# First self-attention: side jobs split over tiles, fewer and larger gathers; cross-attention value and mask jobs at other key tiles

## The reference

```python
x = x + _L0_attn_ref(_layernorm(x), ...)       # 16 heads of 16, ALiBi-like bias
x = x + _L0_xattn_ref(_layernorm(x), ctx_768, mask, ...)   # 8 heads of 64, 1601 keys, masked
x = x + _L0_ffn_ref(_layernorm(x), ...)
x = x + _L1_attn_ref(_layernorm(x), ...)
x = x + _L1_xattn_ref(_layernorm(x), ctx_768, ...)         # 16 heads of 64, 1601 keys
x = x + _L1_ffn_ref(_layernorm(x), ...)

def _L0_attn_ref(x, in_proj_weight, in_proj_bias, out_proj_weight, out_proj_bias):
    qkv = x @ in_proj_weight.T + in_proj_bias
    q, k, v = ...                                # 4 x 16 x 512 x 16 each
    bias = jnp.minimum(rel[None, :, :] * slopes[:, None, None], MAX_BIAS)
    scores = jnp.einsum('bhqd,bhkd->bhqk', q, k) * D ** (-0.5) + bias[None]
    probs = jax.nn.softmax(scores, axis=-1)
    out = jnp.einsum('bhqk,bhkd->bhqd', probs, v)
    return out.transpose(0, 2, 1, 3).reshape(B, S, C) @ out_proj_weight.T + out_proj_bias
```

## Time and profile before

| what | us |
|---|---|
| median of 3 runs (lowest, highest) | 3209.64 (3207.70, 3210.42) |
| the profiled execution | 3209.26 |
| its span, first to last instruction | 3207.5 |
| TensorE busy in the span | 2823.4 (88%) |
| VectorE, ScalarE, GpSimd busy | 1851.7, 1302.5, 1648.4 |
| mean granted TensorE clock | 0.947 |

### The profile page before, as it was taken

How to read it: one execution, slowest core, us unless ns; L and a number is a source line. 1 busy time by engine, 2 the same in 40 slices (tenths; PEclk the granted TensorE clock), 3 DMA queues, 4 the chain that set the end, 5 groups by cost and what they waited for, 6 DMA issues and landing times. The chain is left out here.

```text
span 3207.5 us, 38273 instructions
## 1 busy us (share of the span) xinstructions
PE 2823.4 (88%) x12634; PEld 1744.4 (54%) x12634; DVE 1851.7 (58%) x3753; ACT 1302.5 (41%) x2326; POOL 1648.4 (51%) x1404
## 2 busy tenths in 40 slices
PE   6578786899999999688899999999999999999979
PEld 5333344556565565354655655565556556566457
DVE  2356675566666666536555655555565565565556
ACT  1134554444444454311444444444444444444410
POOL 0344402566566666610466665666666666666710
PEclk8778998999999999898899999999999999999979
DMA  8666513232232322100332232232322233222110
GB/s 266 157 167 151 142 15 90 54 99 67 63 89 64 90 58 56 35 0 22 102 73 49 64 101 49 68 73 58 90 66 67 55 99 75 49 67 63 31 53 27
DMA packets 113532, 245.81 MB, mean 77 GB/s; under 512 B 15366, under 2 KB 61703, under 8 KB 112184
## 3 DMA queue, kind: packets, MB, share of 16 engines
q1 hardware_dynamic: 107128, 219.82, 27.6%
q0 software_dynamic: 5696, 23.42, 2.7%
q10 hardware_dynamic: 512, 0.13, 0.0%
HBM read 107.31 MB, written 31.76 MB: 43 GB/s over the span
## 5 line engine op out<-in xcount | busy, mean ns | idle before, releaser
L1009 POOL TENSOR_TENSOR ACC<-ACC,PR 128x512 f32<-128x512 f32 (+1 forms) x1056 | 1331.1, 1283 | 486.2 <-ACT PR L1234 476.8
L1234 ACT ACTIVATE PR<-banks 128x512 f32<-128x512 f32 (+1 forms) x832 | 469.1, 597 | 682.6 <-PE banks L1123 681.2
L1295 DVE TENSOR_REDUCE mx<-banks 128x2 f32<-128x800 f32 (+1 forms) x512 | 504.2, 986 | 406.8 <-PE banks L1075 405.6
L1139 PE MATMUL banks<-PR,V 128*64 128x512 f32 (+1 forms) x2496 | 602.5, 607 | 0.0
L1122 PE MATMUL banks<-QA,KA 128*128 128x512 f32 (+1 forms) x1248 | 535.4, 429 | 9.7 <-DMA QB<-ROW 8.7
L1075 PE MATMUL banks<-KH,QZ 128*128 128x400 f32 (+1 forms) x1536 | 482.7, 372 | 58.2 <-DVE mx L1295 37.9
L1123 PE MATMUL banks<-QB,KB 65*128 65x512 f32 (+1 forms) x1248 | 495.0, 397 | 0.0
L1075 PEld LDWEIGHTS banks<-KH,QZ 128*128 128x128 f32 x1536 | 268.3, 189 | 246.5 <-issue 113.6
L1234 ACT ACTIVATE PR<-banks,small 128x512 f32<-128x512 f32 (+1 forms) x416 | 269.3, 687 | 306.5 <-PE banks L1123 298.8
L1292 DVE CUSTOM_DVE_ANT_0 banks<-banks,maskadd 128x400 f32<-128x400 f32 (+1 forms) x512 | 289.9, 588 | 158.5 <-PE banks L1075 153.0
L1263 DVE TENSOR_TENSOR KB<-banks,KH 64x400 fp32r<-64x400 f32 (+1 forms) x384 | 219.4, 571 | 261.4 <-ACT KH L1167 255.9
(11 more groups left out here) (240 smaller groups left out, 3047.0 us busy)
## 6 DMA issues: line engine op xcount, KB each, us to landing
KA<-KH SPq DMA_DIRECT2D x192, 400.5 KB, 6.7
CX<-ctx_split SPq DMA_DIRECT2D x8, 2403.0 KB, 10.7
WK<-wk_split SPq DMA_DIRECT2D x48, 256.0 KB, 5.7
WV<-wv_split SPq DMA_DIRECT2D x24, 512.0 KB, 3.6
QA<-QZ SPq DMA_DIRECT2D x96, 128.0 KB, 2.3
QB<-QZ SPq DMA_DIRECT2D x96, 128.0 KB, 2.4
first<-in_w_in SPq DMA_DIRECT2D x8, 1024.0 KB, 6.0
second<-in_w_out1T SPq DMA_DIRECT2D x8, 1024.0 KB, 8.7
```

Source lines behind the costliest of these rows:

```text
L1009: pool.tensor_tensor(acc, other, PR[0:r, n % RING, :], ALU.add).then_inc(summed, 1)
L1139: last = pe.matmul(OB[h * DH:(h + 1) * DH, :], V[0:r, g % 4, s, h * DH:(h + 1) * DH], PR[0:r, (n + h) % RING, :], start=(s == 0), stop=(s ...
L1234: act.activation(PR[0:r, n % RING, :], SB[n % 3][0:r, :], ACT.Exp, bias=keybias[0:r, g // pairs, t:t + 1] if masked else 0.0).then_inc(pro ...
L1295: dve.tensor_reduce(mx[:, :, t, c], couples[i % 2 if g == 0 else 0][:, :, 0:w], AX.X, ALU.max).then_inc(mx_done, 1)
```

## The change

It has six parts.

1. **Jobs split over tiles.** Of a job at tile n, TensorE's part stays at n; ScalarE's copy of the job bank comes one tile later, its rounding to HI two tiles later; VectorE's LO comes four tiles later and its part of v and o jobs two tiles later, and all of VectorE's job parts now stand after the tile's maximum. VectorE normalises at tile 9 of a group and not at 7.
2. **Jobs at other tiles:** p at 0, 4, 20, 29; v at 45, 48; a at 13, 16; o at 32, 36; turn at 7; row at 10. LEAD is 24. The first batch's v jobs stand before its third and fourth p job.
3. **Larger gathers.** The weights' columns are reordered on the host (`paired`), so that the four heads of a half lie side by side. `parts` now has a place for each of the three parts, HI is written twice, and each side of a half is gathered by two transfers of 48 rows, queries first.
4. TensorE's first jobs stand ahead of its wait for the row loads (`self_in`).
5. GpSimd starts to split only after the first group's row has arrived.
6. **Cross-attention:** four value jobs stand at t = 4, 5, 7, 9 and three at 5, 7, 9; the seven stay. The mask steps stand at t = 11 (first), 12 (second and third) and 13 (fourth).

```diff
-        self.parts = nc.dram_tensor("parts", (2, 2, 4, P, S), F32).ap()
+        self.parts = nc.dram_tensor("parts", (2, 4, 2, 3, DH, S), F32).ap()
...
-        HALF = 12 * 16
+        HALF = 4 * 16
...
-                jobs += {1: [("p", b + 1, 0)], 3: [("p", b + 1, 1)], 17: [("p", b + 1, 2)], 19: [("p", b + 1, 3)],
+                jobs += {0: [("p", b + 1, 0)], 4: [("p", b + 1, 1)], 20: [("p", b + 1, 2)], 29: [("p", b + 1, 3)],
...
-                            for side in range(2):
+                            for side, kinds in ((0, "hlh"), (1, "hhl")):
                                 i = 4 * b + 2 * half + side
-                                c = 2 * side + half
-                                sp.wait_ge(lo_ready, i + 1)
+                                to = self.parts[b % 2, 2 * side + half]
                                 if b >= 2:
                                     sp.wait_ge(stacked[half], HALF * (b - 1))
-                                sp.dma_start(self.parts[b % 2, 0, c], raw(HI[:, i % 2, :])).then_inc(hl_out[i % 2], 16)
-                                sp.dma_start(self.parts[b % 2, 1, c], raw(LO[:, i % 2, :])).then_inc(hl_out[i % 2], 16)
-                            for side in range(2):
-                                sp.wait_ge(hl_out[side], 32 * (2 * b + half + 1))
+                                sp.wait_ge(hi_ready, i + 1)
+                                for blk in range(3):
+                                    if kinds[blk] == "h":
+                                        sp.dma_start(to[:, blk], raw(HI[:, i % 2, :])).then_inc(hl_out[i % 2], 16)
+                                sp.wait_ge(lo_ready, i + 1)
+                                sp.dma_start(to[:, kinds.index("l")], raw(LO[:, i % 2, :])).then_inc(hl_out[i % 2], 16)
                             if b >= 2:
                                 sp.wait_ge(sc_ready, PB * (b - 1))
-                            for side, to, parts in ((1, KS, (0, 0, 1)), (0, QS, (0, 1, 0))):
-                                for blk, part in enumerate(parts):
-                                    src = self.parts[b % 2, part, 2 * side + half].rearrange("(i two d) n -> two d i n", two=2, d=D)
-                                    for par in range(2):
-                                        o = DH * par + D * blk
-                                        sp.dma_start(raw(to[o:o + D, b % 2, 4 * half:4 * half + 4, :]), src[par]).then_inc(stacked[half], 16)
+                            for side, to in ((0, QS), (1, KS)):
+                                sp.wait_ge(hl_out[side], 48 * (2 * b + half + 1))
+                                for par in range(2):
+                                    src = self.parts[b % 2, 2 * side + half, par].rearrange("k (d i) n -> (k d) i n", d=D)
+                                    sp.dma_start(raw(to[DH * par:DH * par + 48, b % 2, 4 * half:4 * half + 4, :]), src).then_inc(stacked[half], 16)
...
                     pieces = self.split_pieces()
+                    pool.wait_ge(row_in, 32)
...
+                    for x in before():
+                        job(x)
                     pe.wait_ge(self.self_in, 16 * 8)
                     pe.wait_ge(ones_made, 2)
-                    for x in before():
-                        job(x)
...
-                            act.wait_ge(job_done, i + 1)
-                            act.activation(HI[:, j % 2, :], FULL[:, j % 2, :], ACT.Copy).then_inc(hi_ready, 1)
...
+                    def rounded(x):
+                        j = 4 * x[1] + x[2]
+                        act.wait_ge(job_done, place[x] + 1)
+                        act.activation(HI[:, j % 2, :], FULL[:, j % 2, :], ACT.Copy).then_inc(hi_ready, 1)
...
-                        for x in at(n):
+                        for x in at(n - 2) if n >= 2 else []:
+                            if x[0] == "p":
+                                rounded(x)
+                        for x in at(n - 1) if n >= 1 else []:
                             job(x)
...
-                        for x in at(n):
-                            job(x)
                         if n + LEAD < N:
                             maxima(n + LEAD)
-                        if n % GN == 7 and g >= 1:
+                        for x in at(n - 4) if n >= 4 else []:
+                            if x[0] == "p":
+                                job(x)
+                        for x in at(n - 2) if n >= 2 else []:
+                            if x[0] in "vo":
+                                job(x)
+                        if n % GN == 9 and g >= 1:
...
-            if t >= 4:
-                jobs += values_at(g)[t - 4:t - 3]
+            todo = values_at(g)
+            for x, tile in zip(todo, {0: (), 3: (5, 7, 9), 4: (4, 5, 7, 9), 7: range(4, 11)}[len(todo)]):
+                if tile == t:
+                    jobs.append(x)
...
-                            if masked and g % pairs == 1 and g // pairs + 1 < B and t in (0, 11, 12, 13):
-                                mask_step(g // pairs + 1, (0, 11, 12, 13).index(t))
+                            if masked and g % pairs == 1 and g // pairs + 1 < B:
+                                for c in {11: (0,), 12: (1, 2), 13: (3,)}.get(t, ()):
+                                    mask_step(g // pairs + 1, c)
```

More of the change, by code:

```diff
@@ L403, in self_attention @@
         PB = H * NT
-        LEAD, RING = 22, 8
+        LEAD, RING = 24, 8
         ROWS = 63
         SB, MB, OB, JB = bank[0:3], bank[3:6], bank[6], bank[7]
-        HALF = 12 * 16
+        HALF = 4 * 16
         ident = self.ident
@@ L423, in before @@
         def before():
-            return [("p", 0, i) for i in range(4)] + [("v", 0, 0), ("v", 0, 1)]
+            return [("p", 0, 0), ("p", 0, 1), ("v", 0, 0), ("v", 0, 1), ("p", 0, 2), ("p", 0, 3)]
         def at(n):
@@ L430, in at @@
             if b + 1 < B:
-                jobs += {1: [("p", b + 1, 0)], 3: [("p", b + 1, 1)], 17: [("p", b + 1, 2)], 19: [("p", b + 1, 3)],
-                         34: [("v", b + 1, 0)], 37: [("v", b + 1, 1)]}.get(l, [])
+                jobs += {0: [("p", b + 1, 0)], 4: [("p", b + 1, 1)], 20: [("p", b + 1, 2)], 29: [("p", b + 1, 3)],
+                         45: [("v", b + 1, 0)], 48: [("v", b + 1, 1)]}.get(l, [])
             if b >= 1:
-                jobs += {13: [("a", b - 1, 0)], 15: [("a", b - 1, 1)], 25: [("o", b - 1, 0)], 29: [("o", b - 1, 1)]}.get(l, [])
-            if n % GN == 6 and n >= GN:
+                jobs += {13: [("a", b - 1, 0)], 16: [("a", b - 1, 1)], 32: [("o", b - 1, 0)], 36: [("o", b - 1, 1)]}.get(l, [])
+            if n % GN == 7 and n >= GN:
                 jobs.append(("turn", n // GN - 1, 0))
-            if n % GN == 11 and n // GN + 1 < NG:
+            if n % GN == 10 and n // GN + 1 < NG:
                 jobs.append(("row", n // GN + 1, 0))
@@ L693, in job @@
                             if j >= 2:
-                                dve.wait_ge(hl_out[j % 2], 32 * (j // 2))
+                                dve.wait_ge(hl_out[j % 2], 48 * (j // 2))
                             dve.tensor_tensor(LO[:, j % 2, :], FULL[:, j % 2, :], raw(HI[:, j % 2, :]), ALU.subtract).then_inc(lo_ready, 1)
@@ L1853, in flat, with paired @@
         return g[name].reshape(-1)
+    def paired(w):
+        w = w.copy()
+        w[..., 0:2 * C] = w[..., 0:2 * C].reshape(-1, 4, H // 4, 2, D).transpose(0, 1, 3, 4, 2).reshape(w[..., 0:2 * C].shape)
+        return w
     mask = g["mask_BxS2_bk0"]
@@ L1860, in layouts @@
         "mask": mask, "maskT": padded.reshape(B, KT, P).transpose(0, 2, 1),
-        "w0_in": g["L0_attn_in_proj_weight"].T, "b0_in": g["L0_attn_in_proj_bias"],
-        "b0_cols": g["L0_attn_in_proj_bias"][0:2 * C].reshape(4, P).T,
+        "w0_in": paired(g["L0_attn_in_proj_weight"].T), "b0_in": g["L0_attn_in_proj_bias"],
+        "b0_cols": paired(g["L0_attn_in_proj_bias"])[0:2 * C].reshape(4, P).T,
         "w0_out": g["L0_attn_out_proj_weight"].T, "b0_out": g["L0_attn_out_proj_bias"],
```

4 lines of the change are left out of this document (3 added, 1 removed).

## The result

The changed kernel takes 3235.8 us (median; the kernel before, on the same chip, 3207.9 us): a ratio of 1.0088, with a 95% interval from 1.0063 to 1.0112. It is slower by about 28 us. I had forecast 3227 us. One of its seven executions took 9202.7 us and is left out of the ratio.

The account below looks back on a forecast made before the run. The self-attention tile loop was taken as a chain through three score banks, the cross-attentions as nearly full on TensorE. 3209 us, +48 for self-attention (slow writes in place of a 48 us gain), -30 for cross-attention: 3227 us, 8-in-10 range 3150 to 3285.

Parts of the forecast that it names:

- Two engines: Self-attention's scratch writes of 2x64 rows would run on two DMA engines, 5.5 us a write where it is 0.7.
- The chain of writes sets the last batch's tile 8: Last half of the weights in place at 504 us, making the last batch's tile 8 in self-attention 51 us late.
- two engines, but hidden: Rival: self-attention's slow writes delay only the lead-in, as halves are needed late; 3157 us, chance 0.18.
- All else would be 48 us faster: Lead-in and self-attention loop gain 48 us together if each transfer were as quick as before.
- The lead-in's term: Before the first tile: earlier first projection, earlier gathers, two more maxima ahead; -10 us (-6 to -13).
- The loop's terms: Self-attention tile loop: projections, value and output jobs, turns and row waits, -38 us.
- Turns: Self-attention loop: TensorE no longer stands before a turn for ScalarE's raised outputs; 15 at 0.65 us, -10 us.
- Row waits: Self-attention loop: TensorE's waits for the row transfer beside a gather go; -10 us (-3 to -14).
- Projections: Self-attention loop: the 12 projections inside it delay the tiles less, over three batches; -13 us (-8 to -26).
- The last batch gains 3 us: Self-attention's last batch, from its late tile 8 to the stage's end at 522, gains 3 us.
- Cross-attention: Both cross-attentions: moved mask copy and value jobs give -30 us (-22 to -38).
- what was to show it: Signs: maxima start near 162 us, waits for parts' writes and gathers, last batch's tile 8 near 504, shorter cross-attention groups.

Follow-up runs that it names:

- quick writes: Changed kernel with each write to the scratch tensor cut into two of 64 rows: 3213.8 us, ratio 1.0025 to the kernel before.
- the old rows: Changed kernel with the scratch tensor, writes (128 rows) and gathers (16 rows) of the kernel before: 3203.4 us, ratio 0.9988.
- the early turn: Changed kernel with turn at tile 6, normalise at 7, output jobs at 31 and 34 (were 7, 9, 32, 36): 3217.4 us, ratio 1.0022.
- the kernel with two of its parts: The kernel before with the two cross-attention edits and the lead-in's new job order: 3164.2 us, ratio 0.9867.

## Why the prediction came out as it did

The time is right to 9 us, and so is the sign. But its two large terms are wrong by 74 and 88 us, in opposite directions.

1. *Two engines.* Right: 4 completion packets and 12.7% of 16 engines. The rule of the Trainium skill (DMA: Bandwidth & Descriptors, "Why a DMA increments its semaphore by 16 and not by 1") gives 2 for these writes, and the trace agrees.
2. *The chain of writes sets the last batch's tile 8, +51 us there.* This step failed, although its number looks right: the last half landed at 484.2 us (504 forecast), and the tile is at 497.4 (504 forecast). But with quick writes the loop up to that tile is no shorter, 301.3 us against 299.6. Landing 13 us ahead of its use, the chain ended no wait there. In the profile it shows in the loop as 4.2 us of TensorE's waits, at tile 8 of the first batch, and 4.8 us of ScalarE's, at three of its twelve copies, where I had expected three in each batch. Measured, the writes cost 22 us, all of it in the lead-in (and 42 us by the medians, 30 by the profiled spans, once the tiles are quicker). That is the rival *two engines, but hidden*, which I gave 0.18 and priced at 3157 us. The chain itself was priced fairly: 363 us from the first write to the last landing, where the sum had 380, and 46 us from one half's landing to the next, over the 44 us that I had named as the bound. But I compared it with tiles as quick as before: a batch took 95 to 103 us and not 79, in which two halves of 46 us have room.
3. *All else would be 48 us faster.* Wrong, the larger error: with quick writes I had put 3131 us, and the kernel with writes of 64 rows takes 3213.8. The lead-in's term holds: 164.7 for 173.4 us with the old rows, -8.7 for -10. The loop's terms, -38 us, came out as +50 with quick writes and +40 with the old rows. Turns, -10 us: the wait for RAISED went, as forecast (24.8 us, more than the 10 that I took), and 27.2 us of waiting for normalise took its place, on the same bank, with 20.2 us more at the turns themselves, for projections and output jobs. I had looked at who waits before the turn, and not at who holds its bank before it and who uses it next. Row waits, -10 us: 13.9 us before, over the loop, against 7.9 in the changed kernel, 14.4 with quick writes and 5.3 with the old rows (of the 14.2 us of the view above, 6.3 are ahead of the loop's first tile); a gain isn't shown. Projections, -13 us: +2 us in the loop when made alone at the old tiles, nothing that shows. And I had reckoned no term for the clock: it fell from 0.88 to 0.76 over the loop, and TensorE's busy time rose by 34 us, two thirds of the 50; its waits rose by 16 us, the other third.
4. *The last batch gains 3 us.* It lost 14.6, the clearest case of step 3: no transfers of parts, no projections, 69.5 us at a clock of 0.67; with the early turn 55.4 at 0.94.
5. *Cross-attention, -30 us.* Right: -33. The mask's gap is 4.75 to 4.77 us in every group, and the groups took 47.1 and 46.3 us (47.1 and 46.2 forecast).

Of what was to show it, the maxima began at 161.8 us (162 forecast), and of the waits for writes and gathers the lead-in's came and the loop's hardly did. That the time came out within 9 us was luck: the writes, which I had priced 74 us too high, stood against new tiles, which I had priced 88 us too low. The mechanism that the forecast rests on, a chain of writes that the last batch waits for, is not what made the kernel slower.

What stays open: which of the delays, beside the late turn, brings the clock down in the loop, and whether the clock is the cause outside the last 20 tiles, the only ones in which it was moved by itself.

## What to carry to other kernels

When a job is moved, look at the job that uses its bank or buffer next, and count the distance in tiles from the engine that runs ahead: here one tile between normalise and the row's transpose cost 27.2 us in 14 places, and three tiles cost nothing. An estimate from that: two jobs on one bank need more tiles between them than TensorE's lead plus the delay of the engine that empties it. Price a stall on TensorE twice, by its length and by what the products behind it cost at the lower clock, and test a forecast for a chain of transfers by asking when its last piece is used, not only when it lands. Look at the outermost size of a transfer: writes of 2 x 64 rows ran on two DMA engines here, and those of 64 and of 128 rows on 16. And cut a change in its parts before giving it up: here the kernel with two of its parts is 44 us faster than the one before, and 72 us faster than the one with all of them.

## What the runs showed of the hardware

An issue of a DMA is not always short: with slow writes in the queue, SyncE's instructions for two of them took 9.81 us together, and one took 11.54, where the median with quick writes is 0.6; so a slow transfer also delays whatever its engine would issue next. And added work made TensorE faster: 21 matmuls more in 20 tiles, and 4.0 us less time, with the granted clock at 0.88 and not 0.57 on the mean.
